# Layer 2's routed tiles: the down products and the turned rows one tile later

## The reference, cut to what matters

```
logits = xt @ gate_w.T                     # 8 experts, the best 2 for each token
routed_in = xt[token_idx] * top_scores_sorted[:, None]
for e in range(8):
    h = silu(xe @ w1[e]) * (xe @ w3[e])    # gate and up, 256 -> 256
    out_routed += where(m, h @ w2[e], 0)   # down, 256 -> 256
hs  = silu(xt @ w1s) * (xt @ w3s)          # the shared expert, for all tokens
out = hs @ w2s;  out[token_idx] += out_routed
```

## Time and profile before

| | us |
|---|---|
| median of three executions | 759.71 |
| the profiled execution's own time | 757.46 |
| its span | 755.7 |
| TensorE busy | 701.6 (93%) |
| VectorE busy | 574.0 (76%) |
| ScalarE busy | 484.5 (64%) |
| GpSimd busy | 331.8 (44%) |

### The profile page before, as it was taken

The page is one execution under the profiler, slowest core; times in us unless marked ns, Lnnn a source line. Parts: engine busy times, 40 slices in busy tenths (PEclk is TensorE's granted clock), DMA queues, the critical chain, the costliest instruction groups (busy, mean ns, idle before and its releaser), DMA issues.

```text
span 755.7 us, 14185 instructions
## 1 busy us (share of the span) xinstructions
PE 701.6 (93%) x4989; PEld 622.0 (82%) x4989; DVE 574.0 (76%) x1008; ACT 484.5 (64%) x831; POOL 331.8 (44%) x325
## 2 busy tenths in 40 slices
PE   6899998899999999999999999999899889999994
PEld 6776775678899988999989998999787468898873
DVE  6787777587878778867868786868688867877847
ACT  3477566445567677767767775867567946777740
POOL 6568668402241344135322433232235665777530
PEclk9999999999999999999999999999999899999997
DMA  5000021168568768886867786867470644454438
GB/s 192 1 2 1 1 84 45 51 216 282 172 211 241 264 182 263 253 263 195 264 201 254 238 280 190 253 225 220 112 284 34 222 119 121 143 159 152 131 111 281
DMA packets 58247, 130.63 MB, mean 173 GB/s; under 512 B 6689, under 2 KB 30242, under 8 KB 58178
## 3 DMA queue, kind: packets, MB, share of 16 engines
q1 hardware_dynamic: 46658, 109.09, 41.9%
q0 software_dynamic: 11232, 20.46, 12.2%
q10 hardware_dynamic: 288, 0.19, 0.1%
HBM read 106.90 MB, written 22.81 MB: 172 GB/s over the span
## 4 chain that ended last, share of the span: by engine, by line
PE 64%; DVE 19%; ACT 7%; issue 4%; DMA 3%; POOL 1%; ACTq 1%; DVEq 0%; POOLq 0%; SPq 0%
PE ps L358 56%; DVE w_lo L1353 6%; ACT w_hi L884 2%; PE ps L2482 2%; DVE h_lo L1353 1%; DVE gu L1353 1%; ACT gu L884 1%; DVE hf L2021 1%; PE ps L2439 1%; DVE hf L1796 1%; PE ps L2191 1%; DMA xnb<-y_d 1%; DMA xm_d<-xnb 1%; DVE top_t L1447 1%; ACTq L1271 1%
## 5 line engine op out<-in xcount | busy, mean ns | idle before, releaser
L1353 DVE TENSOR_TENSOR w_lo<-wr,w_hi 128x1024 fp32r<-128x1024 f32 x144 | 175.2, 1222 | 29.0 <-ACT w_hi L884 28.4
L777 POOL DMA_INDIRECT x_d<-ye,sca x39 | 74.5, 1909 | 245.3 <-ACT ye L1060 209.4
L884 ACT ACTIVATE w_hi<-wr 128x1024 fp32r<-128x1024 f32 x144 | 150.7, 1051 | 0.9 <-DMA wr<-in_w 0.9
L358 PE MATMUL ps<-xe_hi,w_hi 128*128 128x256 f32 x480 | 137.4, 286 | 2.0 <-DVE hf L1796 1.8
L358 PE MATMUL ps<-xe_hi,w_lo 128*128 128x256 f32 x488 | 137.8, 283 | 0.0
L358 PE MATMUL ps<-xe_lo,w_hi 128*128 128x256 f32 x480 | 135.8, 283 | 0.0
L358 PEld LDWEIGHTS ps<-xe_hi,w_hi 128*128 128x128 f32 x480 | 92.0, 192 | 5.1 <-DVE xe_lo L1353 3.0
L358 PEld LDWEIGHTS ps<-xe_hi,w_lo 128*128 128x128 f32 x488 | 93.6, 192 | 0.1
L358 PE MATMUL ps<-w_hi,h_hi 128*128 128x256 f32 x312 | 90.9, 291 | 2.6 <-DVE h_lo L1353 2.2
L358 PEld LDWEIGHTS ps<-xe_lo,w_hi 128*128 128x128 f32 x480 | 92.1, 192 | 0.0
L358 PE MATMUL ps<-w_lo,h_hi 128*128 128x256 f32 x312 | 88.2, 283 | 0.0
(11 more groups left out here) (384 smaller groups left out, 1756.9 us busy)
## 6 DMA issues: line engine op xcount, KB each, us to landing
wr<-in_w SPq DMA_DIRECT2D x144, 512.0 KB, 4.8
dr<-in_w1d SPq DMA_DIRECT2D x24, 256.0 KB, 2.7
xn_d<-xnb SPq DMA_DIRECT2D x8, 512.0 KB, 3.3
raw<-in_w1gu SPq DMA_DIRECT2D x8, 512.0 KB, 8.8
x_d<-x_all SPq DMA_DIRECT2D x4, 512.0 KB, 5.5
x_all<-x_d SPq DMA_DIRECT2D x4, 512.0 KB, 4.3
xm_d<-xnb SPq DMA_DIRECT2D x4, 512.0 KB, 4.3
xnb<-y_d SPq DMA_DIRECT2D x4, 512.0 KB, 6.0
```

The costliest lines, as they stand in the source:

```text
L358: return nc.tensor.matmul(out, w, x, start=start, stop=stop, skip_group_check=True)
L777: pool.indirect_dma_start(dst, bass.IndirectOffsetOnAxis(ap=sca[n][:, col + half:col + half + 1], axis=0), ye[:, t % 2, half, :], None, co ...
L884: return s.activation(o, i, ACT.Copy)
L1353: return v.tensor_tensor(o, a, b, ALU.subtract)
```

## The change

In the loop, the down products come two tiles behind gate/up, where they came one tile behind. A single tile's turn comes one tile later too: it stands behind the gate/up of the next tile, and it writes the second half of the down bank of its parity (`4 + p`, columns 256 to 511), which a single tile's down products leave free. For this it waits for `y_ok` of tile t-2, whose sums lay there. ScalarE and VectorE follow: the split of a single tile's turned rows becomes `turned_hi`, `turned_lo` in the next tile's turn; h_hi(t) and h_lo(t) of a double tile move behind gu_hi(t+2), gu_lo(t+2); y1 is called for tile t-2; the down weights of tile t are split in its own turn and no longer one tile ahead. On TensorE the product of the last tile comes behind a first quarter of the shared expert's row group 2.

The diff, whole:

```diff
--- before.py
+++ after.py
@@ -1282,7 +1282,6 @@
             act.wait_ge(raw_in, 16 * E)
             act.wait_ge(r1["eid"], at(r1, "eid") + 1)
             gu_hi(0, expert_of(0))
-            down_hi(0)
 
             def x1_hi(t):
                 n = SPAN[t] * P
@@ -1306,21 +1305,25 @@
                     x1_hi(1)
                 elif t + 2 < T0:
                     x1_hi(t + 2)
+                if t and SPAN[t - 1] == 1:
+                    turned_hi(t - 1)
+                if t + 2 < T0:
+                    gu_hi(t + 2, e)
+                if t >= 2:
+                    y1(t - 2)
                 if SPAN[t] == 2:
                     act.wait_ge(f1["h_mul"], t + 1)
                     copy(h_hi[:, p, :, :].rearrange("p c n -> p (c n)"), hf[:, p, :]).then_inc(f1["h_hi"], 1)
-                else:
-                    act.wait_ge(ht_mm, 2 * SINGLES + SPAN[:t].count(1) + 1)
-                    copy(h_hi[:, p, :, 0:P], ps[:, 2 * p + 1, 0:2 * P].rearrange("p (c n) -> p c n", c=2)).then_inc(f1["h_hi"], 1)
-                if t + 2 < T0:
-                    gu_hi(t + 2, e)
-                if t:
-                    y1(t - 1)
-                if t + 1 < T0:
-                    down_hi(t + 1)
+                down_hi(t)
                 if t == 0:
                     x1_hi(2)
                     shared_hi(1)
+
+            def turned_hi(t):
+
+                p = t % 2
+                act.wait_ge(ht_mm, 2 * SINGLES + SPAN[:t].count(1) + 1)
+                copy(h_hi[:, p, :, 0:P], ps[:, 4 + p, 2 * P:4 * P].rearrange("p (c n) -> p c n", c=2)).then_inc(f1["h_hi"], 1)
 
             act.wait_ge(r1["inv"], at(r1, "inv") + 1)
             shared_hi(0)
@@ -1332,6 +1335,8 @@
             gate_shared(1, 1)
             for t in range(T0):
                 tile1(t)
+            y1(T0 - 2)
+            turned_hi(T0 - 1)
             y1(T0 - 1)
             for g in (2, 3):
                 for i in range(KC):
@@ -2002,7 +2007,6 @@
             normed_lo(2)
             dve.wait_ge(r1["eid"], at(r1, "eid") + 1)
             gu_lo(0, expert_of(0))
-            down_lo(0)
 
             def x1_lo(t):
                 n = SPAN[t] * P
@@ -2017,6 +2021,8 @@
                 if t == 0:
                     e1 = expert_of(1)
                 dve.wait_ge(f1["silu"], t + 1)
+                if t >= 2:
+                    dve.wait_ge(f1["h_lo"], t - 1)
                 up = ps[:, 2 * p + 1, :] if SPAN[t] == 2 else ps[:, 2 * p, D:2 * D]
                 v.tensor_tensor(hf[:, p, 0:n], up, sg[:, p, 0:n], ALU.mult).then_inc(f1["h_mul"], 1)
                 if t == 0:
@@ -2024,24 +2030,29 @@
                     gu_lo(1, e1)
                 elif t + 2 < T0:
                     x1_lo(t + 2)
-                dve.wait_ge(f1["h_hi"], t + 1)
-                if SPAN[t] == 2:
-                    sub(h_lo[:, p, :, :].rearrange("p c n -> p (c n)"), hf[:, p, :],
-                        h_hi[:, p, :, :].rearrange("p c n -> p (c n)")).then_inc(f1["h_lo"], 1)
-                else:
-                    sub(h_lo[:, p, :, 0:P], ps[:, 2 * p + 1, 0:2 * P].rearrange("p (c n) -> p c n", c=2),
-                        h_hi[:, p, :, 0:P]).then_inc(f1["h_lo"], 1)
+                if t and SPAN[t - 1] == 1:
+                    turned_lo(t - 1)
                 if t + 2 < T0:
                     gu_lo(t + 2, e)
                 if t == 0:
                     add_shared(0)
-                if t + 1 < T0:
-                    down_lo(t + 1)
+                if SPAN[t] == 2:
+                    dve.wait_ge(f1["h_hi"], t + 1)
+                    sub(h_lo[:, p, :, :].rearrange("p c n -> p (c n)"), hf[:, p, :],
+                        h_hi[:, p, :, :].rearrange("p c n -> p (c n)")).then_inc(f1["h_lo"], 1)
+                down_lo(t)
                 if t == 0:
                     x1_lo(2)
                     shared_lo(1)
                 if t in (1, 2):
                     add_shared(1, (t - 1,))
+
+            def turned_lo(t):
+
+                p = t % 2
+                dve.wait_ge(f1["h_hi"], t + 1)
+                sub(h_lo[:, p, :, 0:P], ps[:, 4 + p, 2 * P:4 * P].rearrange("p (c n) -> p c n", c=2),
+                    h_hi[:, p, :, 0:P]).then_inc(f1["h_lo"], 1)
 
             shared_lo(0)
             x1_lo(0)
@@ -2050,6 +2061,7 @@
             dve.wait_ge(sgu_mm, KC * 2)
             for t in range(T0):
                 tile1(t)
+            turned_lo(T0 - 1)
 
             def add_last(g):
 
@@ -2735,10 +2747,13 @@
                     transpose1(then or t + 2)
 
             def turn_h1(t):
+                if SPAN[t] == 2:
+                    return
                 p = t % 2
                 pe.wait_ge(f1["h_mul"], t + 1)
+                pe.wait_ge(f1["y_ok"], t - 1)
                 for j in range(2):
-                    ins = T.transpose(ps[:, 2 * p + 1, j * P:(j + 1) * P], hf[:, p, j * P:(j + 1) * P], ident[:, :])
+                    ins = T.transpose(ps[:, 4 + p, (2 + j) * P:(3 + j) * P], hf[:, p, j * P:(j + 1) * P], ident[:, :])
                 ins.then_inc(ht_mm, 1)
 
             def down1(t):
@@ -2772,18 +2787,19 @@
             gate_up1(2)
             pe.wait_ge(so_ok, 3)
             down1(1)
-            turn_h1(2)
             shared_down(1, 1)
             gate_up1(3)
             pe.wait_ge(so_ok, 4)
-            down1(2)
+            turn_h1(2)
             for t in range(4, T0):
                 gate_up1(t)
-                down1(t - 1)
-                if SPAN[t] == 1:
-                    turn_h1(t)
+                turn_h1(t - 1)
+                down1(t - 2)
+            turn_h1(T0 - 1)
+            down1(T0 - 2)
+            shared(2, 0, range(1))
             down1(T0 - 1)
-            shared(2, 0)
+            shared(2, 0, range(1, 2))
             shared(2, 1)
             shared(3, 0)
             shared(3, 1)
```

## The result

The changed kernel took 753.85 us in the median of six executions (750.24 to 754.82), the kernel before 759.33 (756.57 to 762.72): a ratio of 0.9916, 95% interval 0.9894 to 0.9938, so 5.5 us faster. A second set gave 0.9931 (0.991 to 0.9953). The profiled execution took 754.82, its span 753.1.

The account below looks back on a forecast made before the run. TensorE's pauses were taken as the bound. Their removal brings the last scatters 8.0 us earlier, late gathers cost 1.0: 7.0 off the profiled 757.46 gives 750.5, 752.7 against the median; range 749.0 to 758.3.

Parts of the forecast that it names:

- The turns: TensorE in layer 2's loop: seven single tiles' turns stop waiting for hf, 1.08 each, 7.56 us removed.
- The wait before down(1): TensorE's pause of 1.32 us for VectorE's add_shared(1) at the loop's start: 0.5 us removed.
- The wait added at the turn of tile 23: TensorE before down(22): a new wait for hf of 0.95 us, bounds 0 and 1.9.
- The feed: ScalarE and VectorE in the loop keep up with TensorE; margin before gate/up 0.7 us or more, tile 6 0.2.
- rival D: Loop: the ring ScalarE to VectorE stays the bound; minus 0 to 2 us, 758.7; chance 0.12.
- The 0.2 put before down(23): TensorE after the split of shared(2,0): 0.2 us of waiting before down(23) where 0.93 was waited.
- the price of an issue: GpSimd from scatter(1) on: 1.43 us per gather or scatter, making tile 23's transposes 1.0 us late.
- The 12 steps behind scatter(15): GpSimd's issues up to the last scatter, 1.27 us each, so it starts at 721.7 by GpSimd's queue.
- rival C: GpSimd limits more, 1.50 us per issue, last gather 3.1 later: minus 4 us, 755.7; chance 0.17.
- Rival E: GpSimd's long issues become the rule at the last gathers and scatters; slower from u (us per issue) 1.59, 761.2 to 765; chance 0.06.
- The clock: TensorE behind the pause before shared_down(3): possible loss up to 1.1 us, taken as 0, kept for the range.
- The tail: From the last scatter to the end: landing, y_d loads of 6.03 us and add_last stay as before.

Follow-up runs that it names:

- the gathers ahead: Changed kernel with GpSimd issuing three more gathers ahead of scatter(0) and keeping that lead: 750.26 us, 0.9883 of the kernel before; repeats 750.11 and 749.39.
- stores on SyncE: Changed kernel with layer 2's scatters replaced by plain stores from SyncE, rows not placed, output not the reference's: 748.36 us, 0.9871 of the kernel before.
- the small low halves: Changed kernel, VectorE's subtractions with two SBUF inputs cut to 64 columns from tile 4 on, output not the reference's: 749.75 us, 0.9854 of the kernel before.
- The run with the turn in its old place: Changed kernel with gathers three further ahead, single tiles turned right behind their own gate/up in the old bank: 761.01 us, 1.0013 of the kernel before.
- gathers two ahead: Changed kernel with gathers two further ahead and tile 23 turned behind down(22): 752.56 us, 0.9912 of the kernel before.

## Why the prediction was right, and where not

**The turns.** The seven waits of 1.08, minus 7.56 in the sum, are all gone. Eight tiles were put at 31.45; they take 31.4 (gate/up(8) starts at 653.36, gate/up(16) at 684.74). The wait before down(1), 1.32 to be cut by 0.5, is 0.82. The wait added at the turn of tile 23, 0.95 in the sum, is 0.83. Without GpSimd's limit the last scatter was to come 8.0 us earlier; with the gathers ahead it comes 6.6 to 7.7 earlier, and with stores on SyncE 9.0. The TensorE side of the sum held within 1.5 us.

**The feed.** VectorE waits 1.2 us for `gu_hi` where it waited 4.1, and no gate/up waits: rival D is out. The 0.2 put before down(23) came to nothing.

**GpSimd.** The mechanism was named and the start met: scatter(1) was put at 640.7 with a loop that starts at 614.40; it came at 641.94 with one that starts at 615.61, which is the same. The term that was mis-sized is the price of an issue. I took 1.43, the mean of the old stretch; the 46 issues from scatter(1) to scatter(15) took 1.50 and 1.47 in the two profiles of the changed kernel. Over 44 issues that is 3.1 and 1.8 us, and the pauses for gathers came to 3.4 and 2.9 us plus their start-ups, where I had 1.0. The 12 steps behind scatter(15) were priced at 1.27, as if no issue were held there; they took 1.42 and 1.39. So the last scatter, put at 107.3 us after gate/up(0), started at 112.1 and 110.2. The pauses from tile 18 on are the sign that the prediction had named for rivals C and E: in its mechanism the changed kernel is nearer to C, with its 1.50 per issue, than to the forecast. The mean could not be carried over, since it depends on where in a subtraction each issue falls. Against C I had said that the number of subtractions stays the same; fewer issues met one, 28 where it was 33, but with more of it left to run, 0.64 us on average instead of 0.43. Here I also judged the Trainium skill wrongly (SBUF — State Buffer, "Who interferes with whom"), which says that a VectorE instruction with two SBUF inputs contends with GpSimd instructions that read SBUF: I wrote that the trace agrees in kind only and that no issue waits a whole `gu`. Issues wait for what is left of it, up to 1.16 us (the issue from 704.02 to 706.04), and the small low halves show it as a cause. Rival E's rule was the right one, at a smaller price than from u = 1.59 on.

**The clock.** I expected TensorE's pause before shared_down(3) to grow to 2.6 us and looked for a loss of clock behind it. The reverse came: the pause shrank to 1.22, and the products after it ran at full clock. The loss was in the loop, behind the late gather of tile 23: 1.4 us in one of two profiles. The Trainium skill (TensorE: Matmul & The Clock Gate, "Why this matters for your kernels") warns of long pauses between bursts of products; the window at 711.20 shows such a loss behind a pause of 2.01 us, but I had weighed it at one place only.

**The tail.** I took it as unchanged; it is 1.4 to 1.5 us shorter in both profiles. The loads of `y_d` take 4.7 to 4.9 us in all eleven profiles of the changed kernel and its variants, 6.0 and 5.8 in the two with the old order on TensorE, and the issue of four takes SyncE 2.02 to 2.04 us instead of 2.97 and 3.14; all of the difference lies in the second of the four, 0.5 us against 1.44 and 1.61. The run with the turn in its old place has the short tail too (4.75), so it does not come from the turn's place. Why it is shorter is open.

The sum over the two profiles of the changed kernel: the last scatter comes 2.3 and 4.2 us earlier, the tail gives 1.4 and 1.5, and the start of the loop comes 1.2 later, which is scatter between executions (the profiles of all variants have it between 613.95 and 618.27). The medians say 5.5 and 5.9; the forecast was 7.0. That the measured time is so near the forecast is in part luck: without the shorter tail, which was not forecast, the gain would be about 4 us by the medians, an estimate, and that is what rival C gave.

## What to carry to other kernels

Before a stage is made faster, work out the rate of the engine that only feeds it: here GpSimd needed more than the stage's own time for its issues and lived on a lead, and the change both shortened the stage and cut the lead. The lead was won back here by order alone, by moving work that waits for nothing into the idle time ahead of work that waits; in the kernel before, where GpSimd was no limit, the same order brought nothing. A mean duration taken from a stretch with contention holds for that stretch; price it by its two kinds, free and held, by how many are held and by how much of the other engine's work is then left.

## What the runs showed of the hardware

An indirect DMA of 128 rows costs GpSimd 0.97 us, gather and scatter alike, and 0.30 lies between two. One that starts while VectorE runs a subtraction with both inputs in SBUF ends some 0.85 us after that subtraction, 26 of 28 times in the changed kernel; beside a VectorE instruction with an input in PSUM it took at most 1.01, 25 times.

TensorE's clock was at 0.50 for some 3 us after a pause of 2.01 us, and at 1.00 after one of 1.51 in the same place. In the other profiles, from gate/up(0) on, it fell behind pauses of 1.75 (the kernel before) and 2.25 us (gathers two ahead), both ahead of shared_down(3), and not behind pauses of 1.56, 1.66 and 1.73. The length of a pause alone does not tell, though: ahead of the loop, between 600 and 606 us, it fell in every profile behind a pause of 1.5 us or behind one of 1.1 that follows it.
